# Own-key products of two tiles on opposite halves of the array, in a post-LN transformer block

## The reference

```python
q = (x @ Wq).reshape(B, S, 32, 128).transpose(0, 2, 1, 3)
k = (x @ Wk).reshape(B, S, 8, 128).transpose(0, 2, 1, 3)    # each for 4 query heads
v = (x @ Wv).reshape(B, S, 8, 128).transpose(0, 2, 1, 3)
scores = jnp.where(causal, q @ k.T * 128 ** -0.5, -inf)
out = softmax(scores) @ v
x = layernorm(x + out.reshape(B, S, 4096) @ Wo)
base = x @ W_base.T + b_base
weights = sparsemax(x @ W_router.T + b_router)               # 8 experts
h = x @ lora_A                                                # per expert, rank 16
x = layernorm(x + base + (h * weights) @ lora_B)
```

## Time and profile before

| | |
|---|---|
| median of three runs | 680.13 us |
| the profiled execution | 680.35 us |
| its span in the trace | 678.5 us |
| PE busy | 663.3 us, 98% of the span |
| DVE busy | 533.3 us, 79% |
| ACT busy | 412.1 us, 61% |
| POOL busy | 277.0 us, 41% |
| mean granted clock of TensorE | 0.994 of full |

### The profile page before, as it was taken

How to read it: one execution, slowest core, us unless ns; L and a number is a source line. 1 busy time by engine, 2 the same in 40 slices (tenths; PEclk the granted TensorE clock), 3 DMA queues, 4 the chain that set the end, 5 groups by cost and what they waited for, 6 DMA issues and landing times.

```text
span 678.5 us, 11619 instructions
## 1 busy us (share of the span) xinstructions
PE 663.3 (98%) x3606; PEld 355.7 (52%) x3606; DVE 533.3 (79%) x1705; ACT 412.1 (61%) x1071; POOL 277.0 (41%) x423
## 2 busy tenths in 40 slices
PE   7799999999999999999999999999999999999996
PEld 3365555454455555454455555454455545446675
DVE  5989779867888669767898669767788668799875
ACT  1678675666547665667547665667548665657222
POOL 1567970258005841258005841258005630152122
PEclk9899999999999999999999999999999999999999
DMA  9546376345824275354824284255724434554301
GB/s 294 162 103 150 73 156 136 56 94 111 199 45 90 49 176 119 51 99 106 196 48 94 47 190 106 51 97 104 172 47 92 65 61 94 109 126 78 78 33 77
DMA packets 200782, 71.82 MB, mean 106 GB/s; under 512 B 169744, under 2 KB 192784, under 8 KB 200720
## 3 DMA queue, kind: packets, MB, share of 16 engines
q1 hardware_dynamic: 199376, 70.04, 48.2%
q10 hardware_dynamic: 1344, 1.05, 0.6%
HBM read 27.02 MB, written 2.10 MB: 43 GB/s over the span
## 4 chain that ended last, share of the span: by engine, by line
PE 92%; DMA 3%; DVE 2%; issue 1%; SPq 1%; ACT 0%; POOL 0%; DVEq 0%; ACTq 0%
PE bank L1156 23%; PE bank L1107 22%; PE bank L1146 15%; PE bank L1131 13%; PE bank L1119 6%; PE bank L1087 4%; PE bank L1188 3%; DMA pT<-p 2%; PE bank L1090 2%; PE bank L1100 2%; DMA raw<-in_wq 1%; PE bank L1199 1%; PE bank L1211 1%; DVE p L973 1%; PE bank L1176 1%
## 5 line engine op out<-in xcount | busy, mean ns | idle before, releaser
L694 POOL TENSOR_SCALAR raw<-raw,scale_of 128x512 f32<-128x512 f32 x76 | 121.5, 1599 | 126.4 <-ACT wq L756 48.9
L953 DVE CUSTOM_DVE_ANT_0 pr<-bank,mask,back_of 128x32 f32<-128x32 f32 (+15 forms) x256 | 124.4, 495 | 58.2 <-PE bank L1131 56.6
L1107 PE MATMUL bank<-xT,wq 128*128 128x512 f16 x720 | 164.5, 379 | 0.0
L797 ACT ACTIVATE pr<-pr,mx 128x224 f32<-128x224 f32 (+15 forms) x256 | 131.1, 513 | 53.6 <-DVE mx L953 52.4
L806 ACT ACTIVATE p<-pr,ri 128x448 f16<-128x448 f32 (+15 forms) x256 | 117.9, 512 | 60.4 <-DVE ri L964 45.5
L973 DVE SCALAR_TENSOR_TENSOR p<-pr,ri,p 128x256 f16<-128x256 f32 (+15 forms) x256 | 125.4, 533 | 24.5 <-ACT p L806 23.5
L1131 PE MATMUL bank<-kT,qT 128*128 128x32 f16 (+15 forms) x768 | 122.3, 280 | 3.0 <-DVE qT L859 1.9
L1146 PE MATMUL bank<-pT,v 128*128 128x512 f16 x480 | 122.8, 379 | 1.0 <-DMA pT<-p 0.9
L1107 PEld LDWEIGHTS bank<-xT,wq 128*128 128x128 f16 x720 | 70.5, 98 | 82.6
L707 POOL MEMSET p<- 128x192 f16 (+2 forms) x192 | 33.8, 204 | 191.8 <-DMA pT<-p 191.7
L1131 PEld LDWEIGHTS bank<-kT,qT 128*128 128x128 f16 x768 | 66.6, 98 | 60.3 <-issue 3.7
(11 more groups left out here) (121 smaller groups left out, 743.0 us busy)
## 6 DMA issues: line engine op xcount, KB each, us to landing
raw<-in_wo SPq DMA_DIRECT2D x32, 256.0 KB, 3.8
raw<-in_wq SPq DMA_DIRECT2D x30, 256.0 KB, 3.9
raw<-in_wk SPq DMA_DIRECT2D x8, 256.0 KB, 3.1
raw<-in_wv SPq DMA_DIRECT2D x8, 256.0 KB, 3.8
y<-in_x SPq DMA_DIRECT2D x1, 2048.0 KB, 11.1
pT<-p SPq DMA_TRANSPOSE x128, 3.7
out<-y SPq DMA_DIRECT2D x8, 256.0 KB, 2.0
pT<-in_xT SPq DMA_DIRECT2D x6, 256.0 KB, 7.7
```

The lines of the kernel that those rows point to most:

```text
L694: eng.tensor_scalar(raw_of(name, key), raw_of(name, key), scale[0], None, ALU.mult).then_inc(sems["scaled"], 1)
L797: eng.activation(pr[:, t % 2, h, 0:w], pr[:, t % 2, h, 0:w], ACT.Exp, bias=mx[:, k:k + 1], scale=-1.0, accum_out=rs[:, k:k + 1]).then_inc( ...
L953: eng.tensor_tensor_reduce(out=pr[:, t % 2, h, 0:w], in0=psum("S", t, h)[:, 0:w], in1=mask[:, 0:w], scale=score_scale(t), scalar=BIG, op0= ...
L1107: made = eng.matmul(out, wq[:, g % 2, w, h, c * 128:(c + 1) * 128], xT[:, x, c, b * 512:(b + 1) * 512], start=c == 0 and w + x == 0, stop= ...
```

## The change

The own-key product of a tile is cut in two. The high groups (b = 2 and 3) keep 128 keys, as three matmuls of 256 columns (in `PV` t, i). The low groups, also 256 columns, need 64 keys, and go to a new step `PV2` for two tiles 2n and 2n + 1: six matmuls with 64 rows of weights, the even tile's on partitions 64 to 127 and the odd tile's on 0 to 63, one of each in turn, each tile into its own bank. The first and the last pair (tiles 0, 1 and 62, 63; `ALONE`) keep the product of before.

For this the low groups' keys must lie on the right partitions: the rows of `xT` come in a new order (`GROUPS_AT`, `TILE_AT`), even tiles with the reversed order within a tile and odd ones with the natural one, and the mask has two forms in one array. Widths of scores, exp, and halves stay. `pT16` has a place for each tile of four (10,240 numbers a partition, 8,192 before), so a transposing DMA waits for the products of tile t - 4. Both tiles of a pair count as done, and are evicted, behind their `PV2`. All tables of steps are written anew. Which pieces of the first weights and inputs have their lo half made by DVE is changed in three of eight, the mask is filled after `ident`, and there are six warming matmuls for two.

```diff
+TILE_AT = (1, 2, 0, 3)
+ALONE = (0, 31)
+GROUPS_AT = (11, 10, 9, 8, 3, 2, 1, 0, 4, 5, 6, 7, 12, 13, 14, 15)
...
+def completes(name, key):
+    if name == "PV2":
+        return 2 * key[0], 2 * key[0] + 1
+    return (key[0],) if name == "PV" and key[1] == key[0] % NI and key[0] // 2 in ALONE else ()
...
-        elif name == "PV" and key[1] == key[0] % NI:
-            yield ("O_hi", key[0])
-            held.append(("O_lo", key[0]))
+        else:
+            for t in completes(name, key):
+                yield ("O_hi", t)
+                held.append(("O_lo", t))
...
-    ("fetch", "wo", 0, 3), ("most", "k", 0), ("consts",), ("table",), ("most", "x", 0, 1), ("most", "x", 0, 0), ("most", "x", 0, 2), ("warm", 2),
...
-ON_DVE = [("wq", 0, 0), ("wq", 0, 1), ("wv", 0, 0), ("wv", 0, 1), ("x", 0, 2), ("x", 0, 3), ("x", 1, 1), ("x", 1, 3)]
+ON_DVE = [("wk", 0), ("wq", 0, 1), ("wv", 0, 0), ("wv", 0, 1), ("x", 0, 1), ("x", 0, 3), ("x", 1, 1), ("x", 1, 3)]
...
-        pT16 = sb("pT16", [128, 4, 2048], f16)
+        pT16 = sb("pT16", [128, 10240], f16)
...
-        mask = sb("mask", [128, 512])
+        mask = sb("mask", [128, 992])
...
         def group(t, b):
-            return 15 - (4 * (t % NI) + b), 32 * (4 * (t % NI) + b + 1)
+            i = t % NI
+            at = 4 * TILE_AT[i] + (b if i % 2 else 3 - b)
+            return at, (4, 0)[i // 2] if i % 2 else at, 32 * (4 * i + b + 1)
+
+        def own_mask(t, w):
+            return mask[:, 512 - w:512] if t % 2 else mask[:, 480:480 + w]
...
-                    if t >= 2:
-                        sp_.wait_ge(*done("PV", t - 2))
+                    if t >= NI:
+                        sp_.wait_ge(*done("PV", t - NI))
...
                     for a, p in half3:
-                        made = eng.matmul(out, v16[:, a, s, cols], turned_of(t, j, p).rearrange('p a m (h n) -> p a m h n', n=32), start=j == 0 and a + p == 0,
-                                          stop=j == i and a == 1)
-                    if j == i:
+                        if j < i or t // 2 in ALONE:
+                            made = eng.matmul(by_groups(t), v16[:, a, s, cols], turned_of(t, j, p).rearrange("p a m (h n) -> p a m h n", n=32),
+                                              start=j == 0 and a + p == 0, stop=j == i and a == 1)
+                        else:
+                            eng.matmul(by_groups(t)[:, 1], v16[:, a, s, cols], turned_of(t, j, p)[:, 1].rearrange("p m (h n) -> p m h n", n=32),
+                                       start=j == 0 and a + p == 0, stop=False)
+                    if completes(name, key):
                         made.then_inc(sems["PV"], 1)
+                elif name == "PV2":
+                    for a, p in half3:
+                        for t in (2 * key[0], 2 * key[0] + 1):
+                            u, i = divmod(t, NI)
+                            g, b = divmod(u, B)
+                            own = slice(0, 64) if t % 2 else slice(64, 128)
+                            made = eng.matmul(by_groups(t)[:, 0], v16[own, a, v_slot(g // 2, 4 * b + i), (g % 2) * 128:(g % 2) * 128 + 128],
+                                              turned_of(t, i, p)[own, 0].rearrange("p m (h n) -> p m h n", n=32), start=False, stop=a == 1)
+                            if a == 1:
+                                made.then_inc(sems["PV"], 1)
```

More of the change, by code:

```diff
@@ L112 @@
[L112 to L115, removed]
[3 rows of a table removed]
@@ new lines @@
+    ("fetch", "wq", 1, 0), ("exp", 0, 2), ("norm", 0, 0), ("rest", 0, 0), ("inv", 0, 1), ("exp", 1, 2), ("Vp", 0, 0), ("exp", 1, 3), ("S", 2, 0),
+    ("S", 2, 1), ("wq", 0, 2), ("x", 1, 1), ("fetch", "wq", 1, 2), ("norm", 0, 1), ("wq", 0, 3), ("Q_lo", 0, 0), ("Vp", 0, 2), ("rest", 0, 1),
+    ("Q_lo", 0, 1), ("S", 2, 2), ("wq", 0, 1), ("exp", 2, 1), ("most", "k", 1), ("inv", 1, 1), ("K_lo", 0), ("fetch", "wq", 1, 3), ("exp", 1, 1),
+    ("inv", 1, 0), ("Vp", 0, 1), ("K", 1), ("exp", 2, 0), ("Vp", 0, 6), ("fetch", "wq", 1, 1), ("norm", 1, 0), ("norm", 1, 1), ("S", 2, 3),
@@ L128 @@
+    ("exp", 2, 2), ("rest", 1, 1), ("turn", "D"), ("rest", 1, 0), ("exp", 2, 3), ("wo", 0, 2), ("factor", "D"), ("S", 3, 0), ("inv", 2, 1),
[3 rows of a table added]
+    ("fetch", "wv", 1, 1), ("fetch", "wo", 1, 0), ("norm", 3, 0), ("inv", 3, 1), ("factor", ("qk", 1)), ("S", 4, 0), ("norm", 3, 1),
[3 rows of a table added]
+    ("exp", 5, 0), ("most", "o", 1), ("S", 5, 2), ("norm", 4, 0), ("rest", 4, 1), ("Q_lo", 0, 3), ("exp", 5, 1), ("bits", ("ov", 1)), ("PV", 2, 2),
[3 rows of a table added]
 )
 NEXT_STEPS = (
-    ("S", 6, 0), ("fetch", "wk", 2), ("exp", 6, 0), ("wo", 1, 3), ("Q", 2, 1), ("S", 6, 1), ("PV", 4, 0), ("W", 3, 0), ("W", 3, 1),
@@ L176 @@
-    ("inv", 21, 1), ("norm", 21, 1), ("rest", 21, 0), ("W", 18, 3), ("K", 6), ("rest", 21, 1),
+    ("fetch", "wo", 2, 1), ("S", 6, 0), ("fetch", "wq", 2, 1), ("exp", 6, 0), ("PV", 3, 0), ("PV", 3, 1), ("PV", 3, 2), ("wo", 1, 3),
+    ("fetch", "wq", 2, 0), ("fetch", "wq", 2, 3), ("PV", 3, 3), ("S", 6, 1), ("PV2", 1), ("S", 6, 2), ("fetch", "wo", 2, 0), ("fetch", "wk", 2),
+    ("exp", 6, 1), ("exp", 6, 2), ("Q", 2, 1), ("Q", 2, 3), ("inv", 6, 0), ("S", 6, 3), ("exp", 6, 3), ("norm", 6, 0), ("inv", 6, 1), ("rest", 6, 0),
@@ new lines @@
+    ("S", 7, 0), ("norm", 6, 1), ("PV", 4, 0), ("rest", 6, 1), ("Q", 2, 2), ("exp", 7, 0), ("S", 7, 1), ("W", 2, 0), ("fetch", "wq", 2, 2),
+    ("W", 2, 1), ("W", 2, 2), ("wo", 1, 2), ("exp", 7, 1), ("S", 7, 2), ("S", 7, 3), ("exp", 7, 2), ("fetch", "wo", 2, 3), ("inv", 7, 0),
+    ("W", 3, 0), ("fetch", "wo", 2, 2), ("norm", 7, 0), ("S", 8, 0), ("rest", 7, 0), ("exp", 7, 3), ("W", 2, 3), ("exp", 8, 0), ("inv", 7, 1),
+    ("norm", 7, 1), ("most", "k", 2), ("Vp", 1, 0), ("rest", 7, 1), ("W", 3, 1), ("S", 8, 1), ("W", 3, 2), ("S", 8, 2), ("PV", 6, 0), ("S", 8, 3),
@@ new lines @@
+    ("exp", 8, 1), ("W", 3, 3), ("PV", 5, 0), ("PV", 5, 1), ("inv", 8, 0), ("PV2", 2), ("exp", 8, 3), ("S", 9, 0), ("exp", 8, 2), ("PV", 6, 1),
+    ("norm", 8, 0), ("Q", 3, 0), ("most", "q", 2), ("inv", 8, 1), ("bits", ("qk", 2)), ("S", 9, 1), ("norm", 8, 1), ("rest", 8, 0), ("Vp", 1, 1),
+    ("PV", 6, 2), ("S", 9, 2), ("exp", 9, 1), ("exp", 9, 0), ("W", 5, 0), ("W", 4, 0), ("inv", 9, 0), ("W", 4, 1), ("rest", 8, 1), ("W", 4, 2),
+    ("norm", 9, 0), ("S", 9, 3), ("S", 10, 0), ("W", 4, 3), ("most", "o", 2), ("rest", 9, 0), ("turn", ("qk", 2)), ("bits", ("ov", 2)),
@@ new lines @@
+    ("exp", 9, 3), ("exp", 10, 0), ("exp", 9, 2), ("K", 3), ("S", 10, 1), ("W", 5, 1), ("S", 10, 2), ("inv", 9, 1), ("exp", 10, 1), ("norm", 9, 1),
+    ("W", 5, 2), ("rest", 9, 1), ("PV", 7, 0), ("PV", 7, 1), ("exp", 10, 2), ("factor", ("qk", 2)), ("W", 5, 3), ("PV", 7, 2), ("S", 10, 3),
+    ("PV", 7, 3), ("turn", ("ov", 2)), ("exp", 10, 3), ("PV2", 3), ("inv", 10, 1), ("inv", 10, 0), ("norm", 10, 0), ("factor", ("ov", 2)),
+    ("rest", 10, 0), ("norm", 10, 1), ("wq", 2, 1), ("Q", 3, 1), ("S", 11, 0), ("PV", 8, 0), ("rest", 10, 1), ("exp", 11, 0), ("wk", 2),
@@ new lines @@
+    ("S", 11, 1), ("Q", 3, 2), ("W", 6, 0), ("Q", 3, 3), ("S", 11, 2), ("exp", 11, 1), ("exp", 11, 2), ("W", 6, 1), ("S", 11, 3), ("wq", 2, 0),
+    ("W", 6, 2), ("exp", 11, 3), ("inv", 11, 0), ("norm", 11, 0), ("rest", 11, 0), ("inv", 11, 1), ("W", 7, 0), ("PV", 9, 0), ("norm", 11, 1),
+    ("W", 6, 3), ("W", 7, 1), ("S", 12, 0), ("W", 7, 2), ("exp", 12, 0), ("wq", 2, 3), ("PV", 9, 1), ("W", 7, 3), ("S", 12, 1), ("S", 12, 2),
+    ("exp", 12, 1), ("inv", 12, 0), ("rest", 11, 1), ("PV2", 4), ("norm", 12, 0), ("exp", 12, 2), ("Vp", 1, 2), ("wo", 2, 0), ("Q", 4, 0),
[5 rows of a table added]
@@ L177 @@
+    ("exp", 21, 3), ("rest", 21, 0), ("exp", 21, 2), ("W", 16, 3), ("inv", 21, 1), ("norm", 21, 1), ("K", 6), ("rest", 21, 1), ("Q", 6, 0),
 )
 LAST_STEPS = (
[L179 to L181 removed]
@@ new lines @@
+    ("norm", 57, 1), ("rest", 57, 1), ("exp", 58, 0), ("inv", 57, 0), ("norm", 57, 0), ("W", 53, 2), ("S", 58, 3), ("PV", 55, 3), ("rest", 57, 0),
+    ("W", 53, 3), ("lb",), ("exp", 58, 2), ("S", 59, 0), ("Q", 15, 0), ("S", 59, 1), ("S", 59, 2), ("inv", 58, 0), ("exp", 59, 2), ("fetch", "wra"),
+    ("norm", 58, 0), ("PV2", 27), ("rest", 58, 0), ("Q", 15, 1), ("exp", 59, 1), ("exp", 59, 0), ("K", 15), ("W", 54, 0), ("wra",),
+    ("fetch", "wb", 0), ("W", 54, 1), ("exp", 58, 3), ("inv", 59, 0), ("norm", 59, 0), ("W", 54, 2), ("inv", 58, 1), ("W", 54, 3), ("S", 59, 3),
@@ L427, in post_ln_block @@
                 count(f"turned{key[1]}", key[0], by=16)
-            elif name == "PV":
-                if key[1] == key[0] % NI:
-                    count("PV", key[0])
+            elif completes(name, key):
+                for t in completes(name, key):
+                    count("PV", t)
             elif name == "W":
@@ L568, in halves_of_probs, with turned @@
             both = p16[:, b // 2, 0:4 * w].rearrange("p (s m n) -> p s m n", s=2, m=2)
-            return [both[:, s, b % 2, 96 - 32 * b:w] for s in range(2)]
```

(13 more changed lines are left out.)

78 lines of the change are left out of this document (34 added, 44 removed), and 128 rows, old and new, of tables (FIRST_STEPS, LAST_STEPS, NEXT_STEPS).

## The result

The changed kernel takes 684.93 us (median of five runs, 683.09 to 686.56), the kernel before 680.13 us in the same session (679.08 to 682.39, five runs). The ratio is 1.0064, with a 95% interval from 1.0035 to 1.0092: slower by 4.8 us, where 672.0 was forecast and 682.6 was the end of the range. The profiled execution took 685.8 us.

A forecast was written before the change was run, and what follows sets the result against it. TensorE was taken to bound the kernel, its middle streaming at pitch. From 680.35 us, 9.36 less for own-key products and 1.0 more for paired evictions, all else 0, gave 672.0 us; its own range 669.2 to 675.0, the wide one 669.0 to 682.6.

The forecast's parts named there:

- The bound: Middle of the kernel: TensorE streams at its pitch, with at most about 1 us in 153 not streaming.
- The own-key products: 30 pairs of tiles: 64-row matmuls on opposite halves stream together, 312 ns less a pair, 9.36 us less in all.
- The weight loads: Loads for the 64-row matmuls: six take 0.17 us, fit under 0.328 us of streaming and add nothing.
- Turned tiles: Transposing DMAs waiting for tile t - 4, not t - 2: gain between 0 and 0.9 us, none taken.
- The wait for `oT` at tile 58: `W` of tile 58 behind only two scores: TensorE waits at least 0.5 us, about 1 us if ACT or DVE is busy.
- Going to 64 rows and back, 60 times: Changes between 128 and 64 rows around each `PV2`: 0 to 15.7 us over 60 changes, taken as 0.
- The changes cost more than the halves give: Rival: weights at each `PV2` load only into an empty array, 261 ns a change, 687.7 us; chance 0.13.
- The gain is eaten: Rival: both changes of a block empty the array (163 ns each), or halves don't stream together; 681.8 us, chance 0.16.
- One change of each block costs: Rival: only one of a block's two row changes costs, 30 x 0.163 = 4.9 us, 676.9 us; chance 0.15.
- Evictions in pairs: Waits of a tile's `W` for its `oT` when two tiles are evicted together: 0.5 to 3 us, taken as 1.0.
- The start: First weights, inputs and warming matmuls: taken as 0, with 2.2 us either way for TensorE's clock.
- The new order waits: Rival: paired evictions and longer-held banks delay many `W`, 0.2 us at 30 pairs, 6 us, 678 us; chance 0.06.

## Why the prediction was wrong

**Right.** *The bound*: the middle is at TensorE's pitch. *The own-key products*: two halves on other rows stream together, six in the time of three, -9.36 us as computed. *The weight loads* within a block: six in 0.22 us, hidden. *Turned tiles*: nothing. *The wait for `oT` at tile 58*: 0.91 us, forecast 0.5 to 1; but the longest was another, 1.2 us at 167.67 us.

**Wrong, and two thirds of the gain: "Going to 64 rows and back, 60 times", taken as 0.** Measured 1.19 - 0.983 = 0.207 us a block, 0.104 a change, 60 x 0.104 = 6.2 us. It was priced by a change of number type, which isn't a change of rows. The bounds of 0 and 261 ns held it. The measured size is near the 98 ns of a weight load, which stood among them, and below the 163 ns of the matmul's tail; that it is the load is not shown. The Trainium skill, "TensorEngine Tiling (Array Packing)", section Tiling Modes, Key Properties, says that a change of tiling mode drains TensorE. This trace agrees that a change costs, 0.10 us each, which I had weighed and set aside; how much the page doesn't say. Halves and changes together: -9.36 + 6.2 = -3.1 us. Three pairs of kernels with the same order, 64 rows less 128, gave -2.3 (across two sessions), about -4 and -3.0 us. The rival "The changes cost more than the halves give" lies nearest in time (687.7 us), but by luck: it put 261 ns on a change, and at 104 ns, below its own limit of 156, the block gains. "The gain is eaten" had 163 ns, and "One change of each block costs" is out, since both do.

**Wrong in size: "Evictions in pairs", 1.0 us, and "The start", 0.** The order's own cost is 6.5 us less 0.5 for the additional matmuls (128 rows against before), so about 6 where I had 1. I had counted the cover of one kind of wait, `W` for `oT`, at six places. The waits that came are mostly of others: for `hw` 1.8 us and for turned tiles 1.1 in the last steps, maxima 1.1 at 106 us, `qT`, powers and maxima at 60 to 64. They are in tables whose every line was written anew, and I had read them at two places. The rival "The new order waits" had the right size (6 us) and the wrong place: 0.2 us at each of 30 pairs, where from 200 to 600 us there is none and the two ends have nearly all. At the start, the 24 `Vp` took 5.06 us for 4.81, and the next `Vp` began at 38.29 us for 37.46 in the two chains, 0.8 us later.

The sum with measured sizes is 680.35 - 9.36 + 6.2 + 6 = 683.2 us; 684.9 was measured. The 1.7 us between are no more than what the sum leaves out: it takes the order's price from the kernel with 128 rows, where TensorE waits 11.7 us, and in the changed kernel it waits 14.6. One of these waits, 1.2 us of a `W` for `oT` at 167.67 us, isn't in the profile of the kernel with only another last table, whose instructions up to there are the same. So it comes and goes. Of the signs that I had named, the period's came true: it is shorter by 1.1 to 1.4 us and not by 2. Waits for `oT` (2.1 us) and for turned tiles (1.6) each stayed under 3.

**Why the loss.** Not in one rival alone: the half form gains 2 to 4 us by itself, and the order that came with it loses some 6. The order isn't all forced by the change: with another last table 3.0 to 3.4 us come back. But the kernel before gains 1.3 us from the same treatment, and the change in its best order here (681.5) stays behind it (678.9). Not tried: two blocks side by side, so that two pairs of tiles share two changes. By 0.104 us a change I estimate 30 x 0.104 = 3.1 us more from this, but banks would be held longer.

## What to carry to other kernels

- A product on half the rows is priced with its changes of row form: here 0.10 us each way. A block must save more than 0.21 us; three pairs of 256 columns save 0.33 over the same with 128 rows. Splitting a block in two cost 4.5 us; longer blocks should pay, which wasn't tried.
- When all tables of an order are new, run the new order with the old arithmetic first. It splits the result in one experiment, and here the order alone cost 6 us.
- At the ends, where chains of small steps on several engines stand close, read each short cover, not only that of the wait in question.

## What the runs showed of the hardware

- Opposite halves of the rows overlap whatever their order in the program: six 64-row matmuls of 256 columns took 0.43 us in turn and 0.44 us as three of one half and then three of the other. One after another they would take 0.65.
- A change from 128 to 64 rows or back cost 0.10 us, and four changes in place of two cost twice as much (0.41 us for 0.21). In the profile the first load of the new form begins at 197.91 us, when the old form's last matmul has streamed (by 197.82). From float16 to float32, both of 128 rows, four matmuls took 0.87 us, four pitches without that gap.
